# A two-layer graph transformer on one core: the prologue makes k and v of all nodes first, puts the schedule's tables in between, and makes q and skip beside the first gathers

## What is computed

```python
x = layernorm(x + L0(x, edge_attr_64, edge_index))       # x: 6250 nodes x 256, 200000 edges sorted by dst
x = layernorm(x + L1(x, edge_index, edge_weight))
# L0, 4 heads of 32 columns
m = x @ W_n2m.T                                          # 256 -> 128
q, k, v = m @ Wq.T + bq, m @ Wk.T + bk, m @ Wv.T + bv
e = edge_attr @ W_edge.T @ We.T
alpha = softmax over each dst of (q[dst] . (k[src] + e)) / sqrt(32)
out = segment_sum((v[src] + e) * alpha, dst)
x_r = m @ Wskip.T + bskip                                # "skip", xr in the kernel
beta = sigmoid([out, x_r, out - x_r] @ Wbeta.T)
L0 = (beta * x_r + (1 - beta) * out) @ W_m2n.T
```

## Time and profile before

| | us |
|---|---|
| median of 3 runs | 6741.81 (6716.71 to 6789.12) |
| span of the profiled execution, first to last instruction | 4909.6 |
| rest of the median, around the span | 1832.2 |
| prologue (tables, then n0) | 0 to about 122 |
| L0's edge stage | about 122 to 2248 |
| POOL's first gather | 123.28 |

### The profile page before, as it was taken

How to read it: one execution, slowest core, us unless ns; L and a number is a source line. 1 busy time by engine, 2 the same in 40 slices (tenths; PEclk the granted TensorE clock), 3 DMA queues, 4 the chain that set the end, 5 groups by cost and what they waited for, 6 DMA issues and landing times.

```text
span 4909.6 us, 110612 instructions
## 1 busy us (share of the span) xinstructions
PE 3789.0 (77%) x25147; PEld 3208.0 (65%) x25147; DVE 3800.3 (77%) x12902; ACT 2933.3 (60%) x7020; POOL 3298.3 (67%) x3637
## 2 busy tenths in 40 slices
PE   7677777777777777776768888888888887887898
PEld 4566666666666666664546666666666676675787
DVE  4688888888888888886747777767677677776788
ACT  1567776777677677763336666665666665665332
POOL 1777777777777777762367777777777777775455
PEclk9798899899899999898978998989898889899999
DMA  6788888887888888873468888888888888886222
GB/s 199 207 217 214 215 216 216 214 217 213 216 216 215 217 215 212 213 189 94 124 182 227 231 237 233 230 231 234 230 239 232 225 229 237 233 237 188 75 80 66
DMA packets 746042, 996.39 MB, mean 203 GB/s; under 512 B 189632, under 2 KB 503168, under 8 KB 745392
## 3 DMA queue, kind: packets, MB, share of 16 engines
q1 hardware_dynamic: 454336, 481.61, 36.5%
q0 software_dynamic: 150224, 410.39, 31.8%
q10 hardware_dynamic: 140832, 97.33, 6.4%
HBM read 862.96 MB, written 125.90 MB: 201 GB/s over the span
## 4 chain that ended last, share of the span: by engine, by line
PE 26%; DVE 19%; issue 14%; DMA 13%; DVEq 11%; POOL 9%; ACT 3%; ACTq 2%; POOLq 1%; SPq 1%
PE ps L1336 25%; DMA acc_d<-acc 9%; POOL rows L621 8%; DVE score L980 4%; DVE rows L968 3%; DVEq L1192 2%; DVEq L1190 2%; DVE acc L1133 2%; DVEq L1172 2%; DMA dst_row<-in_dst_row 2%; DMA rows<-kv_d,src_all 1%; ACT place L705 1%; DVE msg L1108 1%; ACTq L755 1%; DVE prod L975 1%
## 5 line engine op out<-in xcount | busy, mean ns | idle before, releaser
L621 POOL DMA_INDIRECT rows<-kv_d,src_all x1564 | 1527.6, 977 | 640.1 <-issue 458.5
L621 POOL DMA_INDIRECT rows<-x_d,src_all x1564 | 1484.2, 949 | 540.7 <-issue 440.7
L1336 PE MATMUL ps<-place 128*128 128x256 bf16 (+2 forms) x10560 | 1334.0, 277 | 138.2 <-ACT place L705 134.2
L1336 PEld LDWEIGHTS ps<-place 128*128 128x128 bf16 (+1 forms) x10560 | 1129.7, 140 | 321.9 <-issue 110.7
L701 ACT ACTIVATE place<-dst_row,node_tab 128x512 f32<-128x512 int32 (+1 forms) x880 | 615.4, 710 | 623.4 <-DMA acc_d<-acc 409.7
L1336 PE MATMUL ps<-rows,oh 128*128 x3520 | 882.2, 400 | 59.1 <-DVE oh L1113 33.2
L992 DVE SCALAR_TENSOR_TENSOR prod<-rows,ps 128x256 f32<-128x256 f32 x1760 | 637.3, 418 | 296.0 <-PE ps L1336 188.1
L711 ACT ACTIVATE oh<-iota_row,rel 128x128 f32<-128x128 f32 x2640 | 828.6, 386 | 16.3 <-DMA acc_d<-acc 7.9
L1336 PEld LDWEIGHTS ps<-rows,oh 128*128 128x128 f32 x3520 | 668.6, 198 | 153.3 <-issue 63.1
L1336 PE MATMUL ps<-msg,oh 128*128 128x132 f32 x3520 | 496.1, 287 | 213.5 <-DVE msg L1108 116.1
L705 ACT ACTIVATE place<-place,ones 128x512 f32<-128x512 f32 (+1 forms) x880 | 622.9, 720 | 54.2 <-issue 1.7
(11 more groups left out here) (216 smaller groups left out, 4164.1 us busy)
## 6 DMA issues: line engine op xcount, KB each, us to landing
dst_row<-in_dst_row SPq DMA_DIRECT2D x880, 256.0 KB
place<-q_d SPq DMA_DIRECT2D x440, 192.8 KB
acc_d<-acc ACTq DMA_DIRECT2D x440, 128.5 KB
ea<-in_eaT SPq DMA_DIRECT2D x440, 128.0 KB
acc_d<-acc ACTq DMA_DIRECT2D x440, 66.0 KB
place<-q_d SPq DMA_DIRECT2D x440, 64.0 KB
rows<-kv_d,src_all POOLq DMA_INDIRECT x1564
rows<-x_d,src_all POOLq DMA_INDIRECT x1564
```

Of the source, the lines that this page charges most:

```text
L621: pool.indirect_dma_start(out=L.rows[:, t % SLOTS, j, 0:D], out_offset=None, in_=L.table, in_offset=bass.IndirectOffsetOnAxis(ap=src_all[: ...
L1336: return pe.matmul(out_, lhsT=lhsT, rhs=rhs, start=first, stop=last)
```

## The change

- Three loads that the kv part needs (`w_n2m`, `w_qkvs`, `b_qkvs`) come first, on a semaphore of their own. SP then loads windows 0 to 3, then issues the other 16 loads (`other_loads`, between steps 0 and 2), then window 4 and on.
- The first pass over the 49 windows makes only k and v: a product of 128x256, one DVE instruction, one store on ACT (lag 2 instead of 1). A window has one PSUM bank.
- The table work is cut into four parts that stand between steps 6 and 38 of this pass.
- POOL no longer waits for the phase's end but for the kv stores and the tables, and the first 16 steps are gathered without waiting for scores.
- A second pass over the 49 windows (LB = 3 buffers) loads the nodes again, makes the messages again, and makes q and xr (two products of 128x128, two DVE instructions, a store by SP and one by ACT). The barrier stands behind it for the other four engines.
- `stand_by` becomes `after` in some places of SP, ACT and PE where its argument is a plain number, for which the two are the same.

```diff
+AT_COUNTS, AT_STARTS, AT_PAIRS, AT_LAST = 6, 14, 26, 38
...
+        LB = 3
+        late = [msg_space[:, b * 640:(b + 1) * 640] for b in range(LB)]
...
         @block.sync
...
-            pipeline(sp, (n0_load, -3), (n0_store_q, 1))
-            for b in range(U):
-                sp.wait_ge(n0["store"][b], 48 * turns(b))
+            pipeline(sp, (n0_load, -3), between={1: [other_loads]})
+            sp.wait_ge(s_tab, 1)
+
+            def late_load(w, b, k):
+                wait(n0["m"], before_late(w, b))
+                sp.dma_start(lx[b], a["xT"][:, :, bass.ds(w * P, P)]).then_inc(n0["load"][b], 16)
+
+            def late_store(w, b, k):
+                wait(n0["kv"], NW + w + 1)
+                sp.dma_start(window(q0_d, w), lq[b]).then_inc(n1["store"][b], 16)
+            pipeline(sp, (late_load, -2), (late_store, 1), bufs=LB)
+            for b in range(LB):
+                sp.wait_ge(n1["store"][b], 32 * late_turns(b))
             sp.wait_ge(s_zst, 32)
-            sp.wait_ge(s_tab, 1)
             end_phase(sp, 1)
...
         @block.gpsimd
...
-            end_phase(pool, 1)
-
+            pool.drain().then_inc(s_phase, 1)
+            for b in range(U):
+                pool.wait_ge(n0["store"][b], 16 * turns(b))
+            pool.wait_ge(s_tab, 1)
             pool.wait_ge(s_kept, 16)
...
-                    if t >= LEAD:
+                    if t >= (SLOTS if L is L0 else LEAD):
                         stand_by(pool, gate, s["score"], starts[t - LEAD + 1])
...
         @block.scalar
...
             def n0_store_kv(w, b, k):
                 wait(n0["kv"], w + 1)
                 act.dma_start(node_rows(kv_d, w), nres[b][:, 0:2 * DM]).then_inc(n0["store"][b], 16)
-                act.dma_start(window(xr_d, w), nxr[b][:, :]).then_inc(n0["store"][b], 16)
-            pipeline(act, (n0_messagesT, 0), (n0_store_kv, 1))
+            pipeline(act, (n0_messagesT, 0), (n0_store_kv, 2), between={AT_LAST: [edge_weight]})
+
+            def late_messagesT(w, b, k):
+                wait(n0["m"], NW + w + 1)
+                wait(n0["big"], NW + w - LB + 1)
+                act.activation(lT[b], ps[:, b, 0:P], ACT.Copy).then_inc(n0["mT"], 1)
+
+            def late_store_xr(w, b, k):
+                wait(n0["kv"], NW + w + 1)
+                act.dma_start(window(xr_d, w), lxr[b]).then_inc(n1["store"][b], 16)
+            pipeline(act, (late_messagesT, 0), (late_store_xr, 2), bufs=LB)
             end_phase(act, 1)
...
         @block.vector
...
             def n0_bias(w, b, k):
                 v.wait_ge(n0["big"], w + 1)
-                after(v, n0["store"][b], 48 * k)
-                proj = ps[:, 2 * b + 1, :]
-                v.scalar_tensor_tensor(nbig[b][:, 0:DM], proj[:, 0:DM], OUTC ** -0.5, b_qkvs[:, 0:DM], ALU.mult, ALU.add)
-                v.tensor_tensor(nres[b][:, 0:2 * DM], proj[:, DM:3 * DM], b_qkvs[:, DM:3 * DM], ALU.add)
-                v.tensor_tensor(nxr[b][:, :], proj[:, 3 * DM:4 * DM], b_qkvs[:, 3 * DM:4 * DM], ALU.add)\
+                after(v, n0["store"][b], 16 * k)
+                v.tensor_tensor(nres[b][:, 0:2 * DM], ps[:, b, P:P + 2 * DM], b_qkvs[:, DM:3 * DM], ALU.add)\
                  .then_inc(n0["kv"], 1)
-            pipeline(v, (n0_bias, 1))
+            pipeline(v, (n0_bias, 1), between={AT_COUNTS: [window_counts], AT_STARTS: [starts_of_steps], AT_PAIRS: [pairs_of_steps],
+                                               AT_LAST: [last_pairs, gate_weights]})
+
+            def late_bias(w, b, k):
+                v.wait_ge(n0["big"], NW + w + 1)
+                after(v, n1["store"][b], 32 * k)
+                proj = ps[:, b, P:P + 2 * DM]
+                v.scalar_tensor_tensor(lq[b], proj[:, 0:DM], OUTC ** -0.5, b_qkvs[:, 0:DM], ALU.mult, ALU.add)
+                v.tensor_tensor(lxr[b], proj[:, DM:2 * DM], b_qkvs[:, 3 * DM:4 * DM], ALU.add).then_inc(n0["kv"], 1)
+            pipeline(v, (late_bias, 1), bufs=LB)
             end_phase(v, 1)
...
         @block.tensor
...
+            def n0_messages(w, b, k):
+                pe.wait_ge(n0["load"][b], 16 * (k + 1))
+                after(pe, n0["kv"], w - U + 1)
+                for m in range(2):
+                    i = mm(ps[:, b, 0:P], w_n2m[:, m, :], nx[b][:, m, :], m == 0, m == 1)
+                i.then_inc(n0["m"], 1)
...
+            pipeline(pe, (n0_messages, 0), (n0_project, 1),
+                     between={AT_COUNTS + 2: [window_counts], AT_PAIRS - 2: [pairs_of_steps], AT_LAST: [last_pairs]})
             pe.wait_ge(s_tab, 1)
             pe.wait_ge(s_wc, 1)
...
+            def late_messages(w, b, k):
+                pe.wait_ge(n0["load"][b], late_loads(b, k))
+                after(pe, n0["kv"], before_late(w, b))
...
+            pipeline(pe, (late_messages, 0), (late_project, 1), bufs=LB)
             end_phase(pe, 1)
```

More of the change, by code:

```diff
@@ L232, in build @@
         s_w = sem("weights_loaded")
+        s_w0 = sem("first_weights_loaded")
         s_sched = sem("sched_loaded")
@@ L345, in more, with late_turns, late_loads, before_late @@
             return not (isinstance(c, int) and CH * c + st >= NPAIR)
-        def pipeline(eng, *items):
+        def late_turns(b):
+            return -(-(NW - b) // LB)
+        def late_loads(b, k):
+            return 16 * (turns(b) + k + 1)
+        def before_late(w, b):
+            return NW + w - LB + 1 if w >= LB else U * (turns(b) - 1) + b + 1
+        def stored1(b, k):
+            return 32 * ((late_turns(b) if b < LB else 0) + k)
+        def pipeline(eng, *items, between=(), bufs=U):
             def step(n):
+                for part in between[n] if n in between else ():
+                    part()
                 for item in items:
@@ new lines, in starts_of_steps @@
+            def starts_of_steps():
+                v.wait_ge(s_start, 1)
+                v.tensor_copy(start[:, :], ps[:, 7, P:P + SG])
+                v.drain()
+                for gcol in range(SG):
+                    v.tensor_scalar(begun[:, gcol, :], pair_no[:, :], start[:, gcol:gcol + 1], None, ALU.is_ge)
+                    v.tensor_scalar(stepped[:, gcol, :], pair_no[:, :], start[:, gcol:gcol + 1], d_win[:, gcol:gcol + 1],
+                                    ALU.is_ge, ALU.mult)
+                v.drain().then_inc(s_begun, 1)
@@ L1261, in n1_norm @@
             def n1_norm(w, b, k):
-                after(v, n1["store"][b], 32 * k)
+                after(v, n1["store"][b], stored1(b, k) if k else 0)
                 normal(nres[b][:, 0:D], nh[b][:, :], w, b, roots1[0]).then_inc(n1["x1"], 1)
@@ new lines, in pairs_of_steps, with last_pairs @@
+            def pairs_of_steps():
+                pe.wait_ge(s_begun, 1)
+                for gcol in range(SG):
+                    mm(ps[0:1, 4, gcol * P:(gcol + 1) * P], start[:, gcol:gcol + 1], ident[:, :])
+                for bank, part in ((5, begun), (6, stepped)):
+                    for gcol in range(SG):
+                        i = mm(ps[:, bank, 0:NPAIR], ones[:, :], part[:, gcol, :], gcol == 0, gcol == SG - 1)
+                i.then_inc(s_pairs, 1)
+            def last_pairs():
+                pe.wait_ge(s_w, 16 * N_WEIGHTS)
+                mm(ps[0:DR, 7, 0:DM], w_edge[:, :], w_et[:, :]).then_inc(s_wcp, 1)
+                pe.wait_ge(s_begun, 2)
+                mm(ps[0:1, 4, 0:P], last_pair[:, 0:1], ident[:, :]).then_inc(s_pairs, 1)
@@ L1414, in turn @@
                 def turn(c):
-                    stand_by(pe, gate, s["masked"], c + 1)
+                    after(pe, s["masked"], c + 1)
                     sc = biased[:, :, 0:H].rearrange("p n h -> p (n h)") if H == HEADS else biased[:, :, 0]
@@ L1421, in arrange @@
                 def arrange(c):
-                    stand_by(pe, gate, s["ends"], c + 1)
+                    after(pe, s["ends"], c + 1)
                     mm(arr_ps[0:H, :], sel_h[H][0:R, :], spread[0:R, :, :].rearrange("p m n -> p (m n)"))\
```

233 lines of the change are left out of this document (114 added, 119 removed).

## The result

The changed kernel takes 6827.68 us (median of four runs, 6820.55 to 6859.89); the kernel before, run beside it on the same chip, 6751.0 (four runs, 6716.71 to 6789.12). The ratio is 1.0132, with an interval from 1.0094 to 1.0170: slower, by 77 us between the medians. (The ratios here are not quotients of medians, which would be 1.0114 in this case; as times, this interval is 63 to 115 us.) The forecast was 6789, or +47, and gave "within 1%" most of the chance, 0.76.

A forecast was written before the change was run, and what follows sets the result against it. DVE was taken to set L0's edge stage, POOL 5% below it, behind a serial prologue. An opening 53 us later, less 6 for the ready steps, is +47 on 6741.8: 6789 us, range 6740 to 6830.

The forecast's parts named there:

- The first windows and the first pass: Prologue n0: window 4 near 22 us, 45 windows in 50, tables adding 18, pass ends at 90, POOL starts at 93.
- DVE sets L0's edge stage, and the lead of POOL is worth nothing from step 16: L0's edge stage: DVE keeps 37.6 us a chunk; by step 16 POOL stands where it stood, counted from the opening.
- Rivals 2 and 3: L0's edge stage: 2, the gathers set the pace, 6712 us, chance 0.11; 3, DVE's steady waits go, 6703, chance 0.06.
- rival 2: L0's edge stage: the gathers set it, so POOL's start at 93 instead of 123 counts: 6712 us, chance 0.11.
- The second pass, 78 us at 1.6 a window: Before the barrier: 49 windows of q and xr beside the gathers at 1.6 us each, 78 us (62 to 98).
- The latency loop of 1.27: Second pass: load landing, messages and signals over three buffers, 1.27 us a window, 62 us if uncrowded.
- -6 for the ready steps: First chunk of L0's edge stage: the 16 steps gathered early save about 6 us (0 to 10) of DVE's waits.
- an opening forecast at 175: Start of L0's edge stage on SP, ACT, PE and DVE: 175 us against 121.8, a loss of 53.
- Rival 1: Second pass: gathers crowd it to 2.0 us a window, a loss of 67 us (+76 at 2.2), chance 0.19.
- The 1832.2 us around the span, carried unchanged: Outside the profiled span of 4909.6 us: the rest of the 6741.8 median, 1832.2 us, was taken to stay the same.
- the range that ended at 6830: Whole kernel: predicted time between 6740 and 6830 us, holding the forecast and most of the crowded pass.

The follow-up runs named there:

- a2: The changed kernel, unchanged, run again on a chip of the 4907 kind: 4986.2 us, ratio 1.0157 to the kernel before.
- e1: The changed kernel, but POOL goes through the phase's barrier before its first gather, so nothing is gathered beside the second pass: 4966.5 us, ratio 1.0133.
- e5: e1 with SP's store of q one step later (lag 2 instead of 1), on a chip of the 6800 kind: 6926.7 us, ratio 1.0123.
- e8: e1 with POOL issuing 64 plain loads of kv rows beside the second pass, as many bytes as the 16 early gathers: 4974.9 us, one run.
- e0: The kernel before, unchanged, profiled once more on a chip of the 4907 kind: 4903.5 us, ratio 0.9998.
- a1: The changed kernel, unchanged, run again on a chip of the 6800 kind: 6946.1 us, ratio 1.0135 to the kernel before.
- after: The changed kernel as first measured and profiled, on a chip of the 6800 kind: 6827.68 us, ratio 1.0132 to the kernel before.

## Why the prediction was wrong

**The first windows and the first pass**: right. Window 4 came at 22.45 for "near 22", DVE's last bias of the pass at 96.6 for 90, the first gather at 100.8 (100.0 in a2) for 93. The five to seven us are within the terms' own ranges (43 to 58 for the pass, 14 to 22 for the tables).

**DVE sets L0's edge stage, and the lead of POOL is worth nothing from step 16**: right, on the chip whose trace it was read from. 37.67 us a chunk for 37.61, with the gathers 16 steps ahead or none ahead (e1: first to last score 2062.6 us; before 2060.2; a2 2063.7). Rivals 2 and 3 fall with it. The rule of the Trainium skill that spoke for rival 2 (DMA: Bandwidth & Descriptors, Rules for kernel authors) is to issue a DMA early and to wait late. On the 4907 kind the early issue brought nothing, since the consumer was not held up by the rows.

**The second pass, 78 us at 1.6 a window**: this is the step that failed, in two ways.

- The latency loop of 1.27 left out SP's order of issue. I had written that "SP has little else to issue here, so only their landing counts". SP issues little, but what it issues waits, and what stands behind waits too. Uncrowded the pass takes 1.70 (e1), and 1.39 with the store one step later (e5). The store of q was in the diff, right under the load; what I had seen on ACT ("the copy stands behind the stores") I did not look for on SP.
- For the crowd I took 1.6, nearer to full engines than to the 0.83 of the edge stage. The engines stayed at 0.82 (a2), and a window took 2.16 us beside the gathers, 2.02 over the pass. The wrong argument was "because more DMAs are in flight than there". The engines can be filled (0.99 in e8); this loop doesn't fill them. I suspect the three buffers and SP's order, which bound what SP can have in flight; as said, that is not separated from the share.

The two parts are of about one size against 1.27: 0.43 a window from SP's order and the rest of the uncrowded loop, 0.32 from the gathers. Together the pass and its ends take 105.7 us in a2 (95.0 to 200.7), where I had 85 (90 to 175).

**-6 for the ready steps**: 0. DVE waits for destinations and for SP's signals, 15.4 us before and 15.6 after, beside the first 15; rows from the gathers were not what it waited for, as I had written, and then I counted 6 us for it all the same.

On the 4907 kind this closes the sum: an opening forecast at 175 comes at 200.7, +5 by the first pass and +21 by the second. Before opens at 124.1 (e0), not at the 121.8 that I had set against 175, which was the end of n0's work. So the shift is 76.6, and the time moved by 77.5. Rival 1 had 67, or 76 at 2.2 a window, and it was the nearest; it deserved more than 0.19, since its number was the only one taken from a crowded stretch of the same engines. It was right in part by luck: it laid the whole excess over 1.27 on the crowd, and more than half of it was there without any.

**"The 1832.2 us around the span, carried unchanged"**: wrong. There is nothing around the span but some 2 us. The trace was of the kind on which the kernel takes 4909.6 us, the time of the kind on which it takes 6741.8. A difference of 37% between a span and its own time should have been the first question. The time of 6827.7 lies 2 us inside the range that ended at 6830, and that is luck: the range was built on a sum for another kind of chip. That about +77 came out on both (77.5 and 77 between medians, 111 on the chip of a1) is not a merit of the argument either: on the 6800 kind the second pass takes 156 us for its loads (95.6 to 252.0), 3.3 a window and outside every bound I gave, and the start of the edge stage gives 66 us back.

## What to carry to other kernels

Follow each in-order queue by its own list, not by the conditions of one transfer: a load that could go is held by a store ahead of it that waits for a result. Work moved "beside" another stream, ahead of a barrier, adds its full length there plus what it loses to that stream; the share that a crowded stretch of the same kernel reached (0.83, for 0.82 measured) was a better figure here than full engines, though not a ceiling. And if the span and the time of a profile differ by more than the 2 us seen here within one execution, find out why before anything is added to either.

## What was not expected of the hardware

- **The same program takes 4907 us on some chips and 6750 to 6835 us on others**, with all runs of one occasion alike (19 and 13 of before on two of the chips): of the twelve experiments eight were on chips of the one kind, four on a chip of the other. What makes the kinds is open. The mean granted clock is 0.89 to 0.91 and 0.78 to 0.80. In L0's edge stage a chunk takes 37.67 us in a2 and 54.6 in after (314.43 to 3261.08 in 54). There DVE waits for PE's products ("remote" is a releaser that the trace doesn't name), from the waits of after from 1000 to 1500:

```profile
DVE prod L1036 <- remote: 85.9, 16, 9.5
```

These are 16 of the 74 instructions of L1036 there: in the edge stage most don't wait so for PE. In a2 no wait of DVE in that stretch is longer than 0.6 us.
- **On the 6800 kind products of TensorE are taken up about 10 us late while GpSimd issues indirect gathers**, and at once when it is silent in the second pass (a1, after, e5). The clock is then at its lower level for most of the time (0.57 of full speed from 97 to 183, with PE busy 18 of 86 us; 0.53 in e5 from 172 to 236), but a clock at half speed makes a product of 0.61 us 1.2, not 11. Hand-overs between other engines take 0.03 to 0.05 us on both kinds. Whether the product itself, its write to PSUM or its signal is late the trace doesn't tell, and on a chip of the 4907 kind the same code shows nothing of it. The plain loads of e8, which would have told gathers from traffic, fell on the 4907 kind. The cause stays open.
- The median landing of a 128 KB load was 2.7 us with the engines at 0.55 (e1's shares added up), 3.8 beside the gathers at 0.82 (a2), and 4.7 beside plain loads with the engines at 0.99 (e8).
